# Down projection with 17 instead of 18 matmuls a tile: the weights' low part in the empty half of the last chunk

## The reference

```python
def fp4_linear(x, w):
    xq = fp4_quant_dequant(x)
    wq = fp4_quant_dequant(w)
    return jnp.einsum('bsk,nk->bsn', xq, wq)
gate = fp4_linear(x, w_gate)          # 256 -> 704
y = fp4_linear(x, w_up)               # 256 -> 704
h = jax.nn.silu(gate) * y
return fp4_linear(h, w_down)          # 704 -> 256, the down projection
x = _layernorm(x + attention(x))
x = _layernorm(x + ffn(x))
```

## Time and profile before

| | us |
|---|---|
| median of 3 runs | 745.06 (744.97 to 745.64) |
| the profiled execution, its own time | 742.99 |
| its span, first to last instruction | 741.3 |
| PE busy / PEld busy | 705.2 / 674.0 |
| DVE / POOL / ACT busy | 619.4 / 558.8 / 551.1 |

### The profile page before, as it was taken

The page is one execution under the profiler, slowest core; times in us unless marked ns, Lnnn a source line. Parts: engine busy times, 40 slices in busy tenths (PEclk is TensorE's granted clock), DMA queues, the critical chain, the costliest instruction groups (busy, mean ns, idle before and its releaser), DMA issues.

```text
span 741.3 us, 16606 instructions
## 1 busy us (share of the span) xinstructions
PE 705.2 (95%) x4908; PEld 674.0 (91%) x4908; DVE 619.4 (84%) x1517; ACT 551.1 (74%) x1227; POOL 558.8 (75%) x585
## 2 busy tenths in 40 slices
PE   7999999999999977799999999999999999999984
PEld 5899999888999867799999999999999999999984
DVE  5988999998999977799787787887899887898784
ACT  5677777777888775476777677677677788788777
POOL 4677777777777686687888788788788788787761
PEclk9999999999999999899999999999999999999998
DMA  5222222222222100000000000000000010111113
GB/s 162 60 79 79 72 80 79 66 79 83 68 80 79 43 23 1 1 2 1 1 2 1 2 1 1 2 2 1 1 1 2 15 45 29 44 44 36 53 65 135
DMA packets 40045, 30.04 MB, mean 41 GB/s; under 512 B 3474, under 2 KB 39956, under 8 KB 39956
## 3 DMA queue, kind: packets, MB, share of 16 engines
q1 hardware_dynamic: 37508, 26.75, 11.8%
q10 hardware_dynamic: 2448, 2.23, 1.1%
HBM read 20.58 MB, written 8.39 MB: 39 GB/s over the span
## 4 chain that ended last, share of the span: by engine, by line
PE 83%; issue 6%; DVE 4%; POOL 3%; ACT 2%; DMA 1%; SPq 0%; ACTq 0%; DVEq 0%; POOLq 0%
PE bank L859 63%; PE wide L859 6%; PE wide L970 5%; PE bank L929 3%; PE bank L927 2%; PE wide L916 2%; PE bank L977 2%; PE bank L907 1%; POOL scratch L388 1%; POOL scratch L374 1%; DMA scratch<-L_attn_Wv 1%; POOL scratch L431 1%; PE wide L899 0%; DVE scratch L847 0%; ACT scratch L497 0%
## 5 line engine op out<-in xcount | busy, mean ns | idle before, releaser
L859 PE MATMUL bank<-wf_hi,rounded 128*128 128x352 f32 (+1 forms) x1792 | 402.4, 309 | 12.5 <-DVE wf_lo L742 5.7
L859 PEld LDWEIGHTS bank<-wf_hi,rounded 128*128 128x128 f32 x1792 | 300.3, 190 | 15.6 <-DVE wf_lo L742 5.9
L859 PE MATMUL bank<-wf_lo,rounded 128*128 128x352 f32 (+1 forms) x896 | 273.8, 306 | 0.0
L859 PEld LDWEIGHTS bank<-wf_lo,rounded 128*128 128x128 f32 x896 | 170.3, 190 | 0.0
L431 POOL TENSOR_TENSOR scratch<-scratch 128x704 f32<-128x704 f32 x64 | 94.8, 1482 | 79.5 <-DVE scratch L815 75.9
L859 PE MATMUL bank<-qkv_hi,rounded 128*128 128x512 f32 (+1 forms) x512 | 147.4, 343 | 2.4 <-ACT bank L471 2.4
L416 POOL TENSOR_TENSOR scratch<-scratch 128x704 bf16<-128x704 f32 x64 | 99.4, 1553 | 8.5 <-ACT scratch L610 6.8
L859 PEld LDWEIGHTS bank<-qkv_hi,rounded 128*128 128x128 f32 x512 | 93.1, 191 | 13.2 <-issue 3.4
L380 POOL TENSOR_TENSOR rounded<-scratch,rounded 128x256 fp32r<-128x256 f32 x64 | 46.9, 734 | 58.8 <-ACT rounded L468 58.8
L605 ACT ACTIVATE scratch<-scratch 128x704 uint8<-128x704 f32 x64 | 50.6, 791 | 52.6 <-POOL scratch L431 51.6
L436 POOL TENSOR_TENSOR scratch<-scratch 128x704 f32<-128x704 bf16 x64 | 89.0, 1391 | 0.7 <-DVE scratch L819 0.7
(11 more groups left out here) (102 smaller groups left out, 1505.5 us busy)
## 6 DMA issues: line engine op xcount, KB each, us to landing
scratch<-x_feat SPq DMA_DIRECT2D x64, 128.0 KB, 2.2
scratch<-x_tok SPq DMA_DIRECT2D x64, 128.0 KB, 2.1
out<-scratch SPq DMA_DIRECT2D x64, 128.0 KB, 1.7
scratch<-w_ffn ACTq DMA_DIRECT2D x17, 128.0 KB, 2.2
scratch<-L_attn_Wq SPq DMA_DIRECT2D x1, 256.0 KB, 3.3
scratch<-L_attn_Wk SPq DMA_DIRECT2D x1, 256.0 KB, 3.5
scratch<-L_attn_Wv SPq DMA_DIRECT2D x1, 256.0 KB, 4.9
wo<-L_attn_Wo SPq DMA_DIRECT2D x1, 256.0 KB, 4.1
```

Source lines behind the costliest of these rows:

```text
L859: last = pe.matmul(dst, x(c), w(c), start=first and n == 0, stop=n == len(terms) - 1, skip_group_check=not first)
```

## The change

The last of the six chunks of D had 64 rows of zeros on both sides. Now rows 64 to 127 of the chunk hold, on the side of the weights, the low part of the weights of rows 0 to 63, and on the side of the activations (hqt_hi) a copy of the high part of rows 0 to 63. One matmul then gives high x high and high x low for this chunk, and the matmul with wf_lo for chunk 5 falls away: 17 a tile.

To get there: the last two weight pieces are loaded with two DMAs (192 columns, and the last 64 real columns once more in place of the padding); their low part takes two subtractions, one for columns 0 to 127 into wf_lo, one for partitions 64 to 127 in place in wf_hi. In each tile ACT copies 64 x 128 from `wide` to rows 64 to 127 of hqt_hi, after DVE 829 has read the zeros there (wait for h_lo), and signals h_dup. PE waits for h_dup ahead of the last matmul of D, and ahead of the next transposes into `wide`.

```diff
@@ ACT, attention part: load of the weights
-                        act.dma_start(w_raw, w_ffn.rearrange("j p n -> (j p) n")[bass.ds((i + 1) * P, P), :]
-                                      ).then_inc(ld_w, 16)
+                        if i + 1 < NW - KC:
+                            act.dma_start(w_raw, w_ffn[i + 1, :, :]).then_inc(ld_w, 16)
+                        else:
+                            act.dma_start(w_raw[:, 0:D - TAIL], w_ffn[i + 1, :, 0:D - TAIL]).then_inc(ld_w, 16)
+                            act.dma_start(w_raw[:, D - TAIL:D], w_ffn[i + 1, :, D - P:D - TAIL]).then_inc(ld_w, 16)
@@ ACT, feed-forward part, between line 605 and line 610
+                    if live(i, t, -3):
+                        need(act, h_lo, m - 2)
+                        act.activation(hqt_hi[b1][TAIL:P, IC - 1, :], wide[0:TAIL, (IC - 1) * P:IP],
+                                       ACT.Copy).then_inc(h_dup, 1)
@@ DVE, low part of the weights
+                        piece = bass.ds((i - 1) * P, P)
+                        if i - 1 < NW - KC:
+                            dve.tensor_tensor(wf_lo[:, :, piece],
+                                              w_bank(i)[:, 0:D].rearrange("p (c n) -> p c n", c=KC),
+                                              wf_hi[:, :, piece].bitcast(F32), ALU.subtract).then_inc(w_los, 1)
+                        else:
+                            dve.tensor_tensor(wf_lo[:, 0, piece], w_bank(i)[:, 0:P], wf_hi[:, 0, piece].bitcast(F32),
+                                              ALU.subtract)
+                            dve.tensor_tensor(wf_hi[TAIL:P, 1, piece], w_bank(i)[TAIL:P, P:D],
+                                              wf_hi[TAIL:P, 1, piece].bitcast(F32), ALU.subtract).then_inc(w_los, 1)
@@ PE, transposes into wide
-                        need(pe, h_lo, m - 3)
+                        need(pe, h_dup, m - 3)
@@ PE, down projection
                         three(pd[:, 0:D], lambda c: hqt_hi[b][:, c, :], lambda c: hqt_lo[b][:, c, :],
-                              down(wf_hi), down(wf_lo), IC).then_inc(d_s, 1)
+                              down(wf_hi), down(wf_lo), IC - 1, last=False)
+                        pe.matmul(pd[:, 0:D], hqt_lo[b][:, IC - 1, :], down(wf_hi)(IC - 1), start=False, stop=False)
+                        need(pe, h_dup, m - 3)
+                        pe.matmul(pd[:, 0:D], hqt_hi[b][:, IC - 1, :], down(wf_hi)(IC - 1),
+                                  start=False, stop=True).then_inc(d_s, 1)
```

More of the change, by code:

```diff
@@ L68, in layer_kernel @@
     HALF = I // 2
+    TAIL = I % P
+    assert 2 * TAIL == P
     NB = I // BLK
@@ L216, in layer_kernel @@
             "gua gub sia sib ha hb hmax hs2 hinv hxn hy hmg hc hg hq".split())
-        h_t, h_hi, h_lo, d_s, y_s, y_sq, y_ln, y_o = (
-            sem(f"b_{k}") for k in "ht hhi hlo d y ysq yln yo".split())
+        h_t, h_hi, h_lo, h_dup, d_s, y_s, y_sq, y_ln, y_o = (
+            sem(f"b_{k}") for k in "ht hhi hlo hdup d y ysq yln yo".split())
         block = ctx.enter_context(nc.Block())
@@ L685, in attention @@
                     if t == 3 and live_seq(i, 1, NW):
-                        need(dve, ld_w, 16 * (i + 2))
+                        need(dve, ld_w, 16 * (i + 2 + max(0, i + 2 - NW + KC)))
                         need(dve, w_scs, i + 1)
@@ L853, in _, with three @@
         def _(pe):
-            def three(dst, x_hi_ap, x_lo_ap, w_hi_ap, w_lo_ap, chunks, first=True):
+            def three(dst, x_hi_ap, x_lo_ap, w_hi_ap, w_lo_ap, chunks, first=True, last=True):
                 terms = [(x, w, c) for c in range(chunks)
@@ L858, in three @@
                 for n, (x, w, c) in enumerate(terms):
-                    last = pe.matmul(dst, x(c), w(c), start=first and n == 0, stop=n == len(terms) - 1,
+                    op = pe.matmul(dst, x(c), w(c), start=first and n == 0, stop=last and n == len(terms) - 1,
                                      skip_group_check=not first)
-                return last
+                return op
             pe.wait_ge(consts, 5)
```

## The result

| | before | after |
|---|---|---|
| median, us | 745.21 (743.12 to 745.97, 13 runs) | 746.88 (745.67 to 748.51, 13 runs) |
| the profiled execution, its own time | 742.99 | 747.54 |
| its span | 741.3 | 745.5 |

The ratio is 1.0028, with a 95% interval of 1.0019 to 1.0036. The forecast was 741.5 us, a gain of 3.5; the kernel lost 1.7, so the size was wrong and so was the sign.

What follows compares the result with a forecast made beforehand. PE was taken as the bound in most tiles: +5.70 us for matmuls removed, -0.4 DVE-heavy tiles, -0.1 and -0.3 weights, -1.4 tail, so 3.5 gained and 741.5 us; range 739.6 to 744.4.

Steps and rivals of the forecast that it cites:

- two loops: Steady pair of tiles after the change: PE needs 13.46 us, the loop through ACT, DVE and POOL 13.31 with the copy.
- a step that no row shows: ACT's copy between square and hmg, shifting partitions: taken to add 0.05 us to ACT's path, bounds 0.05 and 0.27.

Runs made afterwards that it cites:

- the late copy: Changed kernel with ACT's copy one step later, ahead of the first silu, read from SBUF, transposes not waiting for it: 742.25 us, ratio 0.9970.
- the seventh: Changed kernel with ACT's copy from hqt_hi in SBUF, partitions 0 to 63, to the same partitions of a spare tile, part of product left out: 744.15 us.

## What to carry to other kernels

An instruction that starts at another partition than its neighbours can cost its full length, and a little more, where rows of neighbours show an overlap; put it where its engine idles anyway, as the late copy did here. When two loops lie within 2% of each other, a step that no row shows must be priced from its dear end. Follow each new wait into the last two tiles, where no queue is full and all that stands behind the wait on its engine is late with it. And where a trace names the releaser of a long pause, ask what would have held the engine without it: of PE's 1.78 us ahead of the last transposes the copy had 0.30, POOL the rest.

## What the runs showed of the hardware

- ACT's overlap of some 0.12 us between neighbours (0.70 against 0.82) is lost to the copy when its input or output starts at partition 64, and to the next instruction that reads or writes the same memory from partition 0 (0.29 to 0.33 against 0.15 to 0.20; silu 0.62 against 0.49). Reads of PSUM and of SBUF count apart: a read at 64 of `wide` held silu three instructions later and not hmg, a read at 64 of hqt_hi held hmg and not silu. It is a rule fitted to six kernels that foretold the seventh; only starts at partitions 0 and 64 were tried.
- The copy of 64 x 128 took 0.27 us on ACT from PSUM and 0.29 to 0.31 from SBUF. On DVE, from SBUF, it took 0.22 with POOL idle and 1.18 on average beside a busy POOL, ending 0.05 to 0.10 after POOL's instruction.
- After 1.78 and 2.23 us without work on PE, with the transposes and one D (2.9 us) between them, the granted clock was 0.55 in the next 3.5 us. After 1.04 and 0.88 us it stayed at 1.00. Pauses of about 1.67 and 2.07 us left it at 1.00 in two kernels and went with 0.66 in a third.
